# Output projection in high and low parts, last batch by token tile, and written-out orders for the first and last turns of a pre-norm attention layer

## The reference, cut to what matters

```python
# x: 8 batches x 256 tokens x 256 channels, float32; 16 heads of 16 channels
x = x + attn(layernorm(x), w_qkv, b_qkv, w_o, b_o)
x = x + layernorm(x) @ w_ste.T + bias

def attn(x, w_qkv, b_qkv, w_o, b_o):
    q, k, v = split(x @ w_qkv + b_qkv)              # per head
    q = q * cos + rotate_half(q) * sin
    k = k * cos + rotate_half(k) * sin
    logits = q @ k.T / sqrt(16), masked to the causal part
    return (softmax(logits) @ v) @ w_o + b_o
# w_ste: weights rounded to -1, 0, 1 times their mean absolute value
```

## Time and profile before

| | us |
|---|---|
| median of 3 runs | 225.9 |
| lowest, highest | 222.73, 230.41 |
| the profiled execution's own time | 221.41 |
| its span | 219.5 |
| mean granted clock of PE | 0.956 |
| busy: PE, DVE, ACT, POOL | 187.5 (85%), 144.3 (66%), 101.9 (46%), 91.8 (42%) |

### The profile page before, as it was taken

The page is one execution under the profiler, slowest core; times in us unless marked ns, Lnnn a source line. Parts: engine busy times, 40 slices in busy tenths (PEclk is TensorE's granted clock), DMA queues, the critical chain, the costliest instruction groups (busy, mean ns, idle before and its releaser), DMA issues.

```text
span 219.5 us, 6069 instructions
## 1 busy us (share of the span) xinstructions
PE 187.5 (85%) x2537; PEld 145.0 (66%) x2537; DVE 144.3 (66%) x272; ACT 101.9 (46%) x146; POOL 91.8 (42%) x154
## 2 busy tenths in 40 slices
PE   7675995779899999999999999999997788967423
PEld 2265873768587778777878778787866556744313
DVE  1489496477488968896789688967884755203311
ACT  2825102536542854483457536663544373573130
POOL 4222220064424934473547256721871373374040
PEclk9889699699999999999999999999999999999965
DMA  6982011001100120022002100210021001001001
GB/s 218 304 279 96 3 48 49 6 0 51 54 0 3 55 97 3 3 73 78 3 0 91 61 0 3 99 51 3 27 73 55 0 3 54 0 0 51 0 0 49
DMA packets 11131, 11.21 MB, mean 51 GB/s; under 512 B 1248, under 2 KB 10592, under 8 KB 11104
## 3 DMA queue, kind: packets, MB, share of 16 engines
q1 hardware_dynamic: 10816, 10.03, 13.8%
q10 hardware_dynamic: 288, 0.79, 1.1%
HBM read 4.39 MB, written 2.10 MB: 30 GB/s over the span
## 4 chain that ended last, share of the span: by engine, by line
PE 71%; DVE 8%; DMA 5%; ACT 5%; issue 4%; POOL 3%; SPq 3%; POOLq 0%
PE score_ps L650 13%; PE pv_ps L733 10%; PE scoret_ps L662 8%; PE c_ps L759 6%; PE score_ps L641 5%; PE a_ps L619 4%; DVE neg_max L503 4%; PE c_ps L578 3%; PE a_ps L621 3%; PE a_ps L620 3%; PE c_ps L771 3%; DMA bias_v<-in_b_v 2%; PE a_ps L632 2%; PE c_ps L746 2%; DMA q_t<-max_t 2%
## 5 line engine op out<-in xcount | busy, mean ns | idle before, releaser
L373 ACT ACTIVATE probs<-scoret_ps 128x1024 f32<-128x1024 f32 x45 | 46.0, 1022 | 59.3 <-PE scoret_ps L662 57.2
L503 DVE TENSOR_REDUCE neg_max<-score_ps 128x4 f32<-128x1024 f32 (+1 forms) x45 | 54.8, 1218 | 18.7 <-PE score_ps L650 18.7
L293 POOL TENSOR_SCALAR_AFFINE_SELECT probs<-probs 128x512 f32<-128x512 f32 (+1 forms) x48 | 38.7, 809 | 48.2 <-ACT probs L373 48.2
L662 PE MATMUL scoret_ps<-q_t,k_t 32*128 32x256 f32 (+1 forms) x480 | 52.3, 346 | 0.0
L650 PE MATMUL score_ps<-k_t,q_t 31*128 31x128 f32 (+1 forms) x480 | 51.4, 343 | 0.0
L662 PEld LDWEIGHTS scoret_ps<-q_t,k_t 32*128 32x128 f32 x480 | 35.5, 187 | 0.7 <-issue 0.5
L650 PEld LDWEIGHTS score_ps<-k_t,q_t 31*128 31x128 f32 x480 | 34.8, 191 | 0.1
L259 POOL TENSOR_SCALAR rstd<-mean_var 128x2 f32<-128x2 f32 x16 | 3.1, 191 | 63.9 <-DVE mean_var L463 63.8
L733 PE MATMUL pv_ps<-probs,v 128*32 128x128 f32 (+1 forms) x512 | 26.0, 330 | 1.4 <-POOL probs L293 1.4
L641 PE MATMUL score_ps<-mask_bf,shift_bf 32*128 32x128 bf16 (+1 forms) x360 | 14.8, 201 | 9.0 <-DVE neg_max L503 4.1
L733 PEld LDWEIGHTS pv_ps<-probs,v 128*32 128x32 f32 x512 | 13.8, 109 | 12.8 <-POOL probs L293 4.3
(11 more groups left out here) (89 smaller groups left out, 340.9 us busy)
## 6 DMA issues: line engine op xcount, KB each, us to landing
xs<-in_L_attn_x SPq DMA_DIRECT2D x8, 256.0 KB, 6.2
q_t<-roped SPq DMA_DIRECT2D x16, 128.0 KB, 2.2
k_t<-roped SPq DMA_DIRECT2D x16, 128.0 KB, 2.1
out_y<-xs SPq DMA_DIRECT2D x8, 256.0 KB, 2.2
wqkv<-in_w_qkv ACTq DMA_DIRECT2D x2, 384.0 KB, 4.1
const<-in_consts SPq DMA_DIRECT2D x2, 256.0 KB, 4.9
wf<-in_w_f SPq DMA_DIRECT2D x1, 256.0 KB, 5.1
wo<-in_w_o SPq DMA_DIRECT2D x1, 256.0 KB, 5.4
```

The source lines that it names most:

```text
L293: nc.gpsimd.affine_select(out=blk, in_=blk, compare_op=ALU.is_ge, fill=0.0, base=0, pattern=[[0, blk.shape[1]], [1, P]], channel_multiplie ...
L373: nc.scalar.activation(probs[m // THIRDS][:, m % THIRDS], scoret_banks(b, m)[:], ACT.Exp).then_inc(exp_done, 1)
L503: nc.vector.tensor_reduce(neg_max[:, t, first:first + 2, heads.start:heads.stop], score_banks(a, m)[:].rearrange("p g (h k) -> p g h k", k ...
L662: made = mm(scoret_banks(b, m)[:, gg, i * width:(i + 1) * width], k_t[b % SLOTS][rows, u, t * P:(t + 1) * P], q_t[b % SLOTS][rows, u, t * ...
```

## The change

The output projection takes its operands in two parts as the other projections do: `attn_high` (ACT) and `attn_low` (DVE) replace `attn_t_copy`, `high_output_weights` (ACT) and `low_output_weights` (DVE) split w_o once, and `attn_project` becomes three fp32r products per pair of tiles, 12 in all. It waits for attn_low.

The steps from attn_transpose on take an argument `part`. For the batches 0 to 6 part 0 is the whole batch in c_ps. For the last batch part 0 and part 1 are its two tiles of 128 tokens, in a0_ps and a1_ps, so each step is called twice with half the size, the store too.

The loop over turns now runs from 3 to 8 on every engine, with another order in it, and what came before and after is written out call by call.

```diff
+        def tiles(c, part):
+            return range(part, part + 1) if c == B - 1 else range(T)
+        def part_bank(c, part):
+            return (a0_ps, a1_ps)[part] if c == B - 1 else c_ps
...
-            def attn_t_copy(c):
-                wait(act, attnt_ps, c + 1)
-                nc.scalar.copy(attn_t[:].rearrange("p c s -> p (c s)"), c_ps[:]).then_inc(attnt_made, 1)
+            def high_output_weights():
+                act.wait_ge(wo_in, 16)
+                nc.scalar.copy(wo_h[:], wo[:]).then_inc(woh_made, 1)
+            def attn_high(c, part):
+                wait(act, attnt_ps, c + part + 1)
+                nc.scalar.copy(attn_h[:, :, tokens(c, part)], channels_first(c, part)).then_inc(attnh_made, 1)
...
+            def low_output_weights():
+                dve.wait_ge(woh_made, 1)
+                nc.vector.tensor_tensor(wo_l[:], wo[:], wo_h[:].bitcast(F32), ALU.subtract).then_inc(wol_made, 1)
+            def attn_low(c, part):
+                wait(dve, attnh_made, c + part + 1)
+                nc.vector.tensor_tensor(attn_l[:, :, tokens(c, part)], channels_first(c, part),
+                                        attn_h[:, :, tokens(c, part)].bitcast(F32), ALU.subtract).then_inc(attnl_made, 1)
...
-            def attn_project(c):
-                wait(pe, attnt_made, c + 1)
-                for t in range(T):
+            def attn_project(c, part):
+                wait(pe, attnl_made, c + part + 1)
+                for t in tiles(c, part):
                     for k in range(C):
-                        last = mm(c_ps[:, t * D:(t + 1) * D], attn_t[:, k, t * P:(t + 1) * P], wo[:, k, :],
-                                  start=k == 0, stop=k == C - 1)
+                        mm(dst, attn_h[:, k, toks], wo_h[:, k, :], start=k == 0, stop=False)
+                        mm(dst, attn_h[:, k, toks], wo_l[:, k, :], start=False, stop=False)
+                        last = mm(dst, attn_l[:, k, toks], wo_h[:, k, :], start=False, stop=k == C - 1)
```

The order on PE, in the opening and in the loop (steps `once(turn == 12, ...)` in the new loops never run):

```diff
-            for turn in range(TURNS):
-                do(turn - 1, v_project)
-                do(turn - 4, xn2_transpose)
...
+            do(0, v_project)
+            do(1, xn_transpose)
+            value_bias()
+            ternary_scale()
+            do(1, qk_project, 0)
+            pair(0, -1, session, 0)
+            for turn in range(3, 9):
+                pair(turn - 3, turn - 4, session, 1)
+                do(turn - 5, attn_transpose, 0)
+                do(turn - 2, qk_project, 1)
+                pair(turn - 3, turn - 4, session, 2)
+                do(turn - 5, attn_project, 0)
+                pair(turn - 3, turn - 4, session, 3)
+                do(turn - 4, values, 0)
+                do(turn - 4, values, 1)
+                pair(turn - 3, turn - 4, session, 4)
+                do(turn - 2, v_project)
+                pair(turn - 3, turn - 4, session, 5)
+                do(turn - 5, xn2_transpose, 0)
+                do(turn - 1, xn_transpose)
+                do(turn - 4, values, 2)
+                do(turn - 3, maxima_transpose)
+                do(turn - 4, values, 3)
+                do(turn - 1, qk_project, 0)
+                do(turn - 5, ternary_linear, 0)
+                pair(turn - 2, turn - 3, session, 0)
+                do(turn - 4, o_transpose)
```

482 lines of the change are left out of this document (353 added, 129 removed).

## The result

The changed kernel takes 212.3 us (median; 209.4 to 214.5), the kernel before 228.2 (222.7 to 232.4) beside it: ratio 0.935, interval 0.918 to 0.952, so it is faster. The forecast was 214.2, range 208.5 to 221.5. The profiled execution is one of the slower ones: own time 214.23, span 212.5, mean clock 0.950. Three others were 210.39 (clock 0.973), 209.39 (0.982) and 209.26 (0.983): the time goes with the mean clock of TensorE.

What follows compares the result with a forecast made beforehand. PE was taken to bound six middle turns, between an opening of waits and a serial end. -4.3 - 3.0 - 0 - 1.1 - 3.3 took span 219.5 to 207.8, own time 209.7; plus 4.5, median 214.2 us, range 208.5 to 221.5.

Steps and rivals of the forecast that it cites:

- Opening, S0(1, 0) at 35.3, gain 4.3: Session 0 scoring batch 1, with batch 0's transposed scores, starts at 35.3 us against 39.56; bounds 1.5 and 5.5.
- fed, PE takes that back: Opening: with work in its wait, PE avoids low clock, where session and projection took 4.2 us against 1.3 + 1.6.
- one of the prediction's own signs of being wrong: Opening: session 0 of batch 1 starting later than 37.5 us would show the prediction wrong.
- My third rival: Opening: first projection still waits for a load or PE falls to low clock; only 1.5 left, 218.6 us; chance 0.08.
- Turns, gain 3.0: From session 0 of batch 1 to 166.22: 123.7 us against 126.7, mostly from the projection half moved into the opening.
- What the projection frees, the waits for maxima take.: Middle turns: 0.42 us saved on PE, but waits of 0.36, 0.25 and 0.2 appear; a turn comes out 0.2 longer.
- Turn (7, 6) and last turn: Turn (7, 6), bound by maxima, stays at 19.6 us; last turn, bound by ACT, 14.8 against 15.9, gain 1.1.
- End, 14.45, gain 3.3: After the last o_transpose, two overlapping 128-token tiles take 14.45 us against 17.8; bounds 1.5 and 4.5.
- From the span to the median: Whole kernel: the earlier median lay 4.5 us above its profiled execution; the same difference turns 209.7 into 214.2.
- The waits did appear: First rival, middle turns: waits for maxima don't appear, saving 0.8 us in four and a half turns; 210.6; chance 0.15.
- DVE became no bound: Second rival, middle turns: DVE becomes the bound, 1.2 us more in each of four and a half turns; 219.6; chance 0.12.
- The fourth: Rival, middle turns: short waits pull PE's clock down, 1.3 us per fall, three in each of five turns; 234; chance 0.03.

Runs made afterwards that it cites:

- the second set: The changed kernel measured once more with no edit: 210.71 us median (209.49 to 212.00), ratio 0.9385.
- the clock held: Changed kernel with products of zeros in the waits of its first two turns: 209.59 us; kernel before with its opening waits so filled: 221.74 us.
- kept warm: Products of zeros in the waits of opening and end, in the kernel before also its last turn: changed kernel 208.68 us, kernel before 217.98 us.

## Why the prediction was right, step by step

**Result.** By its terms the forecast was a span of 207.8 and an own time of 209.7. The executions with the least of the low clock were 209.26 and 209.39, and 209.49 in the second set: 0.2 to 0.4 below. The median forecast, 214.2, was 1.9 too high for a reason of its own, below. That it came so near is in part luck: two executions took 214.2 and 214.5 and three 209.3 to 210.4, and nothing in the sum tells them apart.

**Opening, S0(1, 0) at 35.3, gain 4.3.** Right as to order and DVE, wrong that "fed, PE takes that back". The first projection came at 11.43 (11.5 predicted), session 0 of batch 0 at 20.15 (20.2). With the clock held S0(1, 0) came at 35.18. As the kernel is, it came at 39.27 and 36.86, since the walk left out the waits of 1.47 and more that the new opening itself has, and the clock that falls behind them in these executions. The 39.27 trips one of the prediction's own signs of being wrong (later than 37.5). And the low stretch at 21.3 of the earlier trace rows was no loss to take back: with it filled in the old order, the session still came at 39.83. Against 35.18, the clock held in both, the new order's opening is 4.6 us shorter. My third rival had a clock that falls in the opening as a possibility; it holds for the slower executions, at a price of 1.7 to 4.1 us.

**Turns, gain 3.0.** As run, S0(1, 0) to the turn (7, 6) took 124.5 us (39.27 to 163.76). With the clock held, from S0(1, 0) to the turn (7, 6) 123.6 us (35.18 to 158.8) against 123.7 predicted. The parts were less exact. The first turn took 19.07 with the clock held (19.3). The middle turns took 21.1, not 21.3 (the sign asked for 21.2 to 21.4), and the sixth 20.1, not 19.2. In the middle turn all three waits were overstated: 0.31 for 0.36 at S1, 0.1 for 0.25 at S3, next to none for 0.2 at S4. The projection's saving was too: 0.34 in place of 0.42, because I took 1.51 from a projection with transposes behind it, and one with a session behind it takes 1.59 to 1.62. The sixth turn waited 0.68 before S4, where one group of values had been moved away; I had costed no wait there.

**"What the projection frees, the waits for maxima take."** Right in the sum of a turn, not in the mechanism. In the old order it is so: alone, the projection gave nothing. In the new one it gave 0.32 of its 0.34, and what takes it away is the cost of the order itself, 0.36, with a wait of 0.31 at S1 that stands there without the projection too.

**Turn (7, 6) and last turn.** 19.59 for 19.6; 14.84 for 14.8. The term that I missed here is not in the sum: the new order of the last turn no longer has the waits of 1.01 and 0.71. In the eight profiles of kernels with the new order the step between the last two o_transposes was 15.8 to 16.2 us; in the old order it was 16.9, 17.3, 18.8, 19.6, 16.9 and 17.3, the third and the fourth with the clock down in it (0.74 from 199 to 203, and 0.50).

**End, 14.45, gain 3.3.** 14.31 measured. POOL's second deviation was to end 8.1 us behind the last o_transpose and did (206.33 less 198.19), though the two deviations stood 0.32 apart and not back to back. Without the split the end takes 18.5. A term that the sum does not name is in this: the new projection costs in the end, 0.5 us whole (18.2 against 17.8) and 0.6 split (14.3 against 13.7), since nothing covers attn_low there. The split alone gives 3.9 to 4.0. The float32 projection for the last batch only was not tried.

**From the span to the median.** I added 4.5 us, as the kernel before had between its profiled execution and its median. That step was wrong in kind: the difference is not a constant of the measurement but low clock in the opening and in the last turn, so it changes with the orders. Kept warm, both kernels all but lose it (spreads of 2.3 and 0.6 us).

**What the medians are made of.** 228.2 to 212.3 is 15.9 us; with both kernels kept warm it is 217.98 to 208.68, 9.3. So about 6.5 of the gain in the medians is clock that the new orders lose less of. That is a difference of two differences, with an uncertainty of some 4 us from the spread of the kernel before. By the fastest executions it is less: 222.73 to 209.26 is 13.5, and kept warm 216.98 to 208.52 is 8.5, which leaves 5.0 for the clock.

**Rivals.** The waits did appear, at about half of what I summed (0.44 for 0.81). DVE became no bound in the new order, as the run without half of a maximum shows. The fourth, a clock that falls in the middle turns, did not come: 1.00 there in every profile, with three short waits a turn. Its price per fall, 1.3 us, was too low for some places: the fall in the old order's last turn cost 2.7 (19.60 against 16.93). The rule of the Trainium skill behind it (TensorE: Matmul & The Clock Gate, "A second HAM failure mode: psum-queue depth-cycling") isn't borne out in these turns. And the other rule weighed (VectorE: DVE Perf Modes, "The TRN2 errata — SBUF-src ops pay a fixed extra latency per instruction") holds as to the price, since attn_l (one of its sources lies in PSUM) takes 0.42 on 256 elements and 0.69 on 512, yet decides nothing: the split it speaks against is worth 3.9 us here.

## What to carry to other kernels

A shorter instruction on the busiest engine gives nothing where a chain through a second engine is just as long; look at the distance between two dependent starts, in both kernels, before pricing the instruction. In a serial tail, halves that follow each other through four engines are worth far more than their fixed price (here 3.9 us against 0.14 a split). The same new instruction can pay in one stage and cost in another: the projection gave 0.32 us in a middle turn and cost 0.6 in the tail. And where the runs of one kernel spread by some per cent and the spread goes with the mean clock, look in the profile for the stretch of low clock and the waits ahead of it: cheap products of zeros into a bank that is free take the spread away and show what the order itself is worth.
